# Expert 0 in two tiles of 128 rows, the first of them filled by batches 0 to 5 and computed while batch 7 is still being routed

## What is computed

```python
probs = softmax(x @ gate_w.T); w, idx = top_k(probs, 2); w = w / sum(w)
combine = zeros((T, E)).at[arange(T)[:, None], idx].add(w)
for gup, dn, ce in experts:                 # 8 experts, T = 896 tokens
    g, u = split(x @ gup.T, 2, axis=-1)     # 2 x 1024 columns
    acc += ce[:, None] * (silu(g) * u @ dn.T)
```

## Time and profile before

| | |
|---|---|
| runs shown | 602.05 us median of 3 (599.68 to 603.24) |
| the profiled execution | 603.49 us, its span 601.6 us |
| mean granted TensorE clock | 0.988 |
| TensorE busy | 573.0 us, 95% of the span |
| VectorE, ScalarE, GpSimd busy | 402.7, 313.5, 272.5 us |

### The profile page before, as it was taken

One profiled execution on the slowest core, in us unless ns is written; L12 is line 12 of the kernel. 1 busy time (PEld: TensorE's weight loads), 2 busy tenths in 40 slices (PEclk: granted clock), 3 DMA queues, 4 the chain that ended last, 5 costly groups with the idle time before them and its releaser, 6 DMA issues.

```text
span 601.6 us, 13755 instructions
## 1 busy us (share of the span) xinstructions
PE 573.0 (95%) x5612; PEld 488.8 (81%) x5612; DVE 402.7 (67%) x819; ACT 313.5 (52%) x601; POOL 272.5 (45%) x238
## 2 busy tenths in 40 slices
PE   7989999999989999999999999999899999999994
PEld 6767677777756887988888888867899999989994
DVE  7785577678686565667666676667586777746651
ACT  2434554555555556555565555544445567636641
POOL 4338468559641064546555564640300344421324
PEclk9989999999999999999999999998899999999998
DMA  7910480000000000000000000037172677636112
GB/s 233 360 45 3 173 322 2 2 3 1 3 2 1 2 1 2 9 1 24 17 9 17 9 25 1 23 130 307 32 232 85 233 244 254 211 71 225 30 20 25
DMA packets 23803, 50.93 MB, mean 85 GB/s; under 512 B 7040, under 2 KB 16560, under 8 KB 20400
## 3 DMA queue, kind: packets, MB, share of 16 engines
q1 hardware_dynamic: 18272, 45.20, 20.7%
q0 software_dynamic: 4224, 3.70, 3.4%
q10 hardware_dynamic: 1232, 1.01, 0.6%
HBM read 37.89 MB, written 13.31 MB: 85 GB/s over the span
## 4 chain that ended last, share of the span: by engine, by line
PE 83%; DVE 9%; POOL 3%; ACT 2%; issue 2%; DMA 1%; POOLq 0%; ACTq 0%; DVEq 0%
PE ps L59 14%; PE ps L60 13%; PE ps L61 13%; PE ps L736 5%; PE ps L705 5%; PE ps L718 4%; PE ps L593 4%; DVE KN L1103 4%; PE ps L574 3%; PE ps L665 3%; PE ps L655 2%; PE ps L609 2%; POOL sr L1796 2%; PE ps L553 2%; PE ps L485 1%
## 5 line engine op out<-in xcount | busy, mean ns | idle before, releaser
L1841 POOL TENSOR_SCALAR P<-P,rinv 112x487 f32<-112x487 f32 x56 | 84.5, 1521 | 62.7 <-DVE rinv L1136 62.5
L60 PE MATMUL ps<-XGf,WH 128*128 128x256 f32 x252 | 71.3, 283 | 0.0
L61 PE MATMUL ps<-XGf,WL 128*128 128x256 f32 x252 | 71.3, 283 | 0.0
L59 PE MATMUL ps<-XGf,WH 128*128 128x256 f32 x252 | 71.3, 283 | 0.0
L1796 POOL TENSOR_TENSOR sr<-sv,mhalf 125x32 f32<-125x32 f32 x13 | 70.7, 5436 | 1.1
L406 POOL DMA_INDIRECT out<-WS,rows_i x16 | 28.4, 1776 | 89.1 <-ACT WS L1696 85.7
L1103 DVE TENSOR_REDUCE KN<-ps 112x4 f32<-112x1500 f32 x32 | 55.0, 1717 | 19.2 <-PE ps L574 19.2
L1451 DVE TENSOR_TENSOR WL<-WR,WH 128x1024 fp32r<-128x1024 f32 x48 | 57.1, 1220 | 13.4 <-ACT WH L1750 9.8
L1612 ACT ACTIVATE P<-ps,nm 112x487 f32<-112x487 f32 x64 | 42.1, 663 | 45.4 <-DVE nm L1128 41.8
L1563 ACT ACTIVATE P<-ps 125x1344 f32<-125x1344 f32 x32 | 41.3, 1292 | 42.1 <-PE ps L593 42.1
L1128 DVE TENSOR_REDUCE nm<-ps 112x1 f32<-112x487 f32 x64 | 39.5, 658 | 17.3 <-PE ps L705 17.3
(11 more groups left out here) (268 smaller groups left out, 1556.8 us busy)
## 6 DMA issues: line engine op xcount, KB each, us to landing
WR<-in_gupT SPq DMA_DIRECT2D x16, 1024.0 KB, 6.6
WR<-in_dwnT SPq DMA_DIRECT2D x8, 1024.0 KB, 10.1
xs<-ZT SPq DMA_DIRECT2D x14, 516.0 KB, 5.7
CT<-in_ctxT SPq DMA_DIRECT2D x1, 2250.0 KB, 10.3
P<-xs SPq DMA_DIRECT2D x7, 256.0 KB, 10.7
P<-xs SPq DMA_DIRECT2D x9, 128.0 KB, 2.6
Wk<-in_L_xattn_Wk SPq DMA_DIRECT2D x2, 512.0 KB, 11.9
Wv<-in_L_xattn_Wv SPq DMA_DIRECT2D x2, 512.0 KB, 12.0
```

What stands on the lines that cost most here:

```text
L59: e.matmul(out, ah, bh, start=start, stop=False)
L60: e.matmul(out, ah, bl, start=False, stop=False)
L61: return e.matmul(out, al, bh, start=False, stop=stop)
L1841: e.tensor_scalar(P[:, k, 0:487], P[:, k, 0:487], rinv[:, k:k + 1], None, ALU.mult).then_inc(s("psc"), 1)
```

## The change

Expert 0 no longer runs as a pair of tiles. Its first tile is the first 128 rows of its stretch of `xs`. After batch 5 its count is raised to at least 128 (one VectorE instruction), so that later rows fall behind these; the scatters of batches 0 to 5 and of 6 and 7 have a semaphore each. SP loads the first tile when the former have landed (`early`, ahead of the loads of expert 1's weights in its queue). The tile's stages stand in the attention's order: `tx` (transposes, copy and low part), `tg` (four groups of six products of 512 columns, the rows stationary), `ts` (silu and product), `tt` (transposes back, copy and low part), `td` (24 products of 256 columns) and the scaled copy out. The second tile takes the same stages at the head of the expert part, with expert 1's transposes between them and expert 1's first unit ahead of its `td`. Expert 0's and expert 1's splits all move into the attention's order; pieces 3, 4 and 5 of expert 0's low parts go to GpSimd. The fillers of the former tail are gone, and 20 stand ahead of the second tile's transposes. The tables `PAIR_LAST`, `TAIL1`, `TAIL_NEXT` and `TAIL_LAST` have new times. Some semaphores are merged.

```diff
@@ tables
-SPLIT = ((10.5, "split", 0), (18, "low", 0), (38, "split", 1), (38.1, "split", 2), ...
+LOW_POOL = (3, 4, 5)
+SPLIT = ((7.66, "split", 0, 0), (10.03, "low", 0, 0), (10.22, "split", 0, 1), (12.31, "low", 0, 1),
...
+CUT, TILE = 6, 128
+EARLY = ((24.98, "tx"), (27.34, "tg", 0, 0), (29.62, "tg", 0, 1), (33.68, "tg", 1, 0), (37.84, "tg", 1, 1),
+         (33.8, "ts", 0), (35.59, "ts", 1), (42.7, "tt", 0), (48.77, "tt", 1), (93.43, "td"))
-WARM = {("kp", 0, 1, 0): 36, ("spk", 0, 2): 30, ("xt", NB - 1, 3): 18, ("rt4", NB - 1): 26, ("xin", 0): 62,
-        ("up", 0, 0): 10}
+WARM = {("tx", 1): 20, ("kp", 0, 1, 0): 36, ("spk", 0, 2): 30}
@@ expert_order
-    put("xin", 0)
+    put("tx", 1)
+    put("tg", 1, 0, 0)
+    put("tg", 1, 0, 1)
+    put("ts", 1, 0)
+    put("xin", 1)
+    put("tg", 1, 1, 0)
+    put("tg", 1, 1, 1)
+    put("ts", 1, 1)
+    put("tt", 1, 0)
+    put("pair", 2)
...
             put("up", x, dc)
+            if i == 0:
+                put("tt", 1, 1)
+                put("td", 1)
@@ TensorE, in tensor_first
+            if stage == "tx":
+                if t_ == 0:
+                    w.wait_ge(s("xg_early"), 16)
+                    w.wait_ge(s("aT1"), NB)
...
+                w.wait_ge(s("txh"), t_ + 1)
+                to = ps[:, 2 * q + part, :]
+                for z in range(2):
+                    o = z * 2048 + part * 1024 + q * 512
+                    w.wait_ge(*split_done(0, o // 1024))
+                    for W_ in W:
+                        e.matmul(to, XGTo[:, 0, z * 128:(z + 1) * 128], W_[:, o:o + 512],
+                                 start=(z == 0 and W_ is W[0]), stop=False)
+                w.wait_ge(s("txl"), t_ + 1)
...
         def tensor_experts(e, w):
-            w.wait_ge(s("prob"), 2 * NPAIR)
...
+            w.wait_ge(s("yc0"), 1)
@@ VectorE
+                if b == CUT - 1:
...
+                    e.tensor_scalar(base_[:, j, 0:1], base_[:, j, 0:1], float(TILE), None, ALU.max).then_inc(s("cut"), 1)
...
-            w.wait_ge(s("scatter"), 32 * NB)
-            for c in range(LATE_LOW, 4):
-                split_low(e, w, 0, c)
@@ GpSimd
+                elif stage == "low" and i[0] == 0 and i[1] in LOW_POOL:
+                    split_low(e, w, *i).then_inc(s("wl_pool"), 1)
@@ SP
+                elif stage == "early":
+                    w.wait_ge(s("scatter_a"), 32 * CUT)
+                    e.dma_start(XGe, xs[0:TILE, 0:D]).then_inc(s("xg_early"), 16)
+                    e.dma_start(EX[:, 0, 0, :], xs[0:TILE, D:ROW]).then_inc(s("wt_early"), 16)
```

More of the change, by code:

```diff
@@ L131 @@
          (22.8, "v1c", 2), (27.27, "v1c", 3))
[L132 to L146, removed]
+TAIL1 = ((12.93, "aT"), (13.76, "wo"), (14.9, "res", 3), (16.9, "stats", 3), (19.68, "norm", 3), (21.15, "xt", 3),
+         (20.64, "xtc", 3), (22.92, "rt0"), (23.2, "rt1"), (29.67, "rt2"), (32.6, "rt3"), (35.43, "rt4"),
+         (35.93, "rt5"))
@@ new lines @@
+TAIL_NEXT = ((13.99, "aT"), (16.94, "wo"), (16.89, "res", 3), (17.76, "stats", 3), (19.2, "norm", 3),
+             (24.91, "xt", 3), (23.91, "xtc", 3), (30.15, "rt0"), (24.95, "rt1"), (27.97, "rt2"), (28.8, "rt3"),
+             (33.27, "rt4"), (37.21, "rt5"))
+TAIL_LAST = ((-2.49, "rv"), (2.14, "rb"), (3.86, "rbc"), (3.57, "aT"), (13.1, "wo"), (9.19, "res", 3),
+             (10.9, "stats", 3), (12.24, "norm", 3), (16.34, "xt", 3), (16.47, "xtc", 3), (19.16, "rt0"),
+             (16.73, "rt1"), (18.97, "rt2"), (20.56, "rt3"), (28.06, "rt4"), (31.34, "rt5"))
@@ L216, in expert_order @@
     put = order.put
-    for x in range(2):
-        for c in range(3):
-            put("load", x, c)
+    for c in range(3):
+        put("load", 0, c)
+    put("early")
+    for c in range(3):
+        put("load", 1, c)
     put("pair", 0)
@@ L224, in expert_order @@
         put("load", 2, c)
-    put("xin", 0)
-    units = [(x, dc) for x in range(NE) for dc in range(4)]
+    put("tx", 1)
[8 more added lines that the diff above has]
+    put("pair", 2)
+    units = [(x, dc) for x in range(1, NE) for dc in range(4)]
     for i in range(len(units) + 2):
@@ L230, in expert_order @@
             put("up", x, dc)
-            if dc == 0 and x:
+            if i == 0:
+                put("tt", 1, 1)
+                put("td", 1)
+                put("rows", 0)
+                put("sent", 0)
+                put("over", 0)
+                put("oversent", 0)
+                put("ahead", 1)
+                for c in range(3):
+                    put("load", 3, c)
+            if dc == 0 and x > 1:
                 put("split", x, 5)
@@ L845, in tensor_experts @@
                         count.append(count_of(e, w, x))
[L846 to L850, removed]
+                    j, banks = x % 2, pair_banks(stage, x, dc)
+                    pair_free(w, stage, x, dc)
                     w.wait_ge(*pair_done("xin", x))
-                    for part in range(u == 1, 2):
+                    for part in range(2):
                         for c2 in range(2):
@@ L884, in tensor_experts @@
                     x, = i
+                    if x == 0:
+                        count.append(count_of(e, w, x))
                     with e.If(count[x] > 256):
@@ L918, in pairs_out @@
         def pairs_out(w, x):
+            w.wait_ge(s("ttl"), 4)
             before = [pair_use[q] for q in moe.entries[:moe.entries.index(("over", x))] if q in pair_use]
-            for k in range(3):
-                w.wait_ge(s(f"pair{k}"), 1 + max(u // 3 for u in before if u % 3 == k))
+            for k in range(4):
+                w.wait_ge(s(f"pair{k}"), max([n for j, n in before if j == k], default=0))
         def sent_before(w, x, k):
             if k:
-                w.wait_ge(s(f"far_y{x}"), 16 * k)
+                w.wait_ge(s("far_y"), 64 * x + 16 * k)
             else:
```

337 lines of the change are left out of this document (222 added, 115 removed).

## The result

| | before | after |
|---|---|---|
| time, median of 8 runs each | 601.94 us (599.68 to 603.62) | 606.27 us (604.69 to 609.54) |
| ratio, 95% interval | | 1.0093, 1.0068 to 1.0117 |
| the profiled execution, its span | 603.49, 601.6 us | 608.78, 607.0 us |

The change makes the kernel slower by 4.3 us; the prediction was 598.5. The profiled execution of after is 2.5 above its median, so its rows show one of the bad cases.

A forecast was written before the change was run, and what follows sets the result against it. It took the chain of waits from the last attention product (418.00) to expert 0's first (440.09) as the bound. Dense work gave gain 448.35 - t; with t 444.9, 3.5 us off the 602.05 median: 598.5, range 596.5 to 600.5.

The forecast's parts named there:

- rival 3: GpSimd's three 3.0 us pieces and VectorE exclude each other: half blocked 603.1, in full 607.6; chance 0.12.
- both of its signs: Signs that the forecast is wrong: t past 447, and VectorE's low parts over 1.22 us beside GpSimd's.
- t: Time of the second tile's first product, taken as 444.9; the change gains 448.35 - t.
- How much work leaves the dense part: From the second tile's first product to expert 2's transposes: 18.26 us, so without delay the gain would be 8.2.
- (a) to (c): Chain through batch 7's norm and routing: row numbers 4.6 us late, scatters landed at 440.7, t not before 443.9.
- 1.0 that I had added for `td`'s clock: Allowance for the early tile's down products partly at half clock, moving t from 443.9 to 444.9.
- (b): Batch 7's norm to its first routing instruction: VectorE's 3.04 us outlasts TensorE's 1.40 us group; routing starts at 428.4.
- (d): Early tile's down products, fillers and transposes: t 443.7 at full clock, up to 2.9 us more at half speed.
- GpSimd's pieces: Three low parts of expert 0 on GpSimd, priced 3.0 us each from bounds of 2.9 and 3.2.
- What costs nothing: ScalarE's four splits, GpSimd's low parts, expert 1's rows, the count's `max` and merged semaphores: covered or small.
- rival 2: Gain lost to late early rows or earlier batches' tails stalling TensorE (3 us): 601 to 602; chance 0.21.
- Rival 1: VectorE's additions hide in waits: row numbers 1.5 us late, t about 441.5, gain 6.8, time 595.2; chance 0.17.

The follow-up runs named there:

- e5: The changed kernel with GpSimd's three two-input subtractions replaced by one-input multiplications of the same columns, those low parts left out: 601.99 us, ratio 0.9985 to 1.0018.
- e9: The changed kernel with VectorE/GpSimd instruction pairs measured ahead of it: VectorE's two-SBUF-input instruction took 2.00 us beside a subtraction, 0.74 multiplication, 0.68 copy, 0.42 base.
- e12: The kernel before, with only three GpSimd multiplications of 1024 columns added in the places of the change's three pieces: 602.48 us, ratio 0.9987 to 1.0021.
- e2: The changed kernel with piece 3 of expert 1's low parts moved behind batch 7's row numbers on VectorE: 606.51 us, ratio 1.0048 to 1.0078.
- e3: The changed kernel with GpSimd's pieces on VectorE, expert 1's last three low parts behind the scatters' landing, 8 last fillers for 20: 601.82 us, ratio 0.9976 to 1.0011.
- e4: The changed kernel with 20 fillers added on TensorE ahead of the early tile's second group of transposes: 608.61 us, ratio 1.0061 to 1.0131.
- e10: The changed kernel with pieces 3 and 4 on VectorE and only piece 5 left on GpSimd: 605.10 us, ratio 1.0031 to 1.0067.
- e7: e3 with batch 7's row numbers put directly behind its choice on VectorE: 601.34 us, ratio 0.9974 to 1.0012.

## Why the prediction was wrong, by its steps

**The step that failed is the weighing of one row against rival 3.** Rows 9 showed a two-input VectorE instruction inside one of GpSimd, not held up, and I took this for GpSimd in general. That instruction of GpSimd is a multiplication, the one form that lets VectorE through (e5, e9, e12); the change adds subtractions. I did note that no row showed two two-input instructions together, and still gave the case 0.12. What the runs show in its place: beside a subtraction of 1024 columns VectorE's two-input instruction takes 2.00 us instead of 0.42 (e9), its low part 3.70 instead of 1.22 (after), and the form alone makes 4.3 us (e5). Rival 3 had the mechanism: VectorE's chain was blocked for 6.1 us in the profiled execution, past the 3.5 at which it said that blocking decides, and both of its signs came (t at 453.2, past 447; low parts of 2.85 and 3.70). That its range, 603.1 to 607.6, holds the median 606.3 is in part luck. It adds the blocking to a 598.5 that was itself 3.5 us too low, as e5 shows (602.0 without the blocking), and the clock that fell behind the blocking is not in it. Of the 7.8 us between 598.5 and 606.3 the blocking with what follows from it explains 4.3.

**How much work leaves the dense part:** 18.26 predicted, 18.67 measured (453.16 to 471.83). Nearly right. That the clock may be low at its start, 1.6 us more, was missed; it happened in e2, e3, e4 and e10.

**(a) to (c), the chain to the row numbers.** Norm 7 was to end at 425.4 and ended at 429.9, the routing was to start at 428.4 and started at 433.9, the first row numbers were to come at about 436.0 and came at 443.9. With the multiplication in the subtractions' place (e5) root 6 to the first product is 32.3 us; the prediction's 444.9 - 413.6 is 31.3. Up to the end of the first row number it is 23.2 in e5 and 22.4 in the sum, so VectorE's additions were right within 1 us. Behind it two errors nearly cancel, by luck: the scatter's 1.25 (2.19 for 0.94, in e5 too), which I did not have, and 1.0 that I had added for `td`'s clock, while e5's TensorE waits 1.47 for the rows and `td` is not on its path. VectorE's low parts behind the row numbers had no price in my sum, since nothing in VectorE's queue waits for them, but they hold up GpSimd.

**(b), the clock.** That TensorE's clock falls earlier, behind the wait for norm 6, was not foreseen. The six products ahead of `rt0 7` took 2.7 us at a granted clock of 0.50 instead of 1.40, and VectorE waited 1.08 for them.

**(d)** `td` at half speed was foreseen (2.9 to 5.8 us); it took 5.3. In after it ended 0.3 ahead of the rows' path, with its fillers; it decided only when the rest was mended (e7).

**GpSimd's pieces** take 2.35 us, not 3.0: both my bounds were too high, the time per column of a multiplication is no bound for a subtraction.

**What costs nothing:** the earlier batches' tails cost 0.8 us (aligned), a quarter of what rival 2 allowed. Rival 2's early rows were in time: their load was issued at 410.7 and landed 2.0 later, and their transposes at 421.30 waited for VectorE. Rival 1 did not come about.

What e5 gives against before is less than its path says: 32.3 against 34.7, less 0.4 in the dense part and 0.8 to 1.2 up to root 6, leaves about 1 us of gain, and none was measured. So of the 3.5 us by which the forecast was off without any blocking, about 2.5 are found (1.0 between root 6 and t, 0.4, 0.8 to 1.2), and 1 stays open.

## What to carry to other kernels

An idle GpSimd is not free help for a busy VectorE: before work is moved there, list what VectorE runs beside it, and let that be instructions that read PSUM or reduce (unchanged beside all three forms in e9). A row shows the absence of a conflict only for its own two forms. And low-priority work directly behind the instruction that releases a scatter is not free either: put it behind the landing. Last, a chain that is shortened brings the clock of the idle engine onto the path, so fillers that cost nothing before are worth trying again.

## What was not expected of the hardware

- GpSimd's instruction on SBUF holds VectorE up by form: a 1024-column subtraction (2.34 us) and copy (1.04 us) until they end, a multiplication (2.77 us) by 0.2 to 0.3 us, 0.7 in e12. On GpSimd the copy is 2.7 times as fast as the multiplication.
- VectorE's instruction that began first is not always safe: the low part at 437.86 began 0.26 before GpSimd's piece and took 3.70. But in e4 the low part at 417.16 began 0.07 before GpSimd's pair and took its usual 1.21, while the pair took 5.69 instead of 4.71. The order of the starts in the trace does not tell which of the two waits.
- A scatter's issue on GpSimd (0.94) is held up by VectorE's subtractions in SBUF for as long as they follow one another: 2.22 beside two, 3.35 beside three, 0.94 beside none. The Trainium skill, in the section named above, infers that a `tensor_tensor` does not hold up the making of descriptors; in these rows the whole issue is held up; which part of it waits they do not show.
- The granted clock between 24 and 44 us is 0.91 in some profiled executions and 1.00 in others, though all these programs do the same there. With it the landmark at 44.1 moves by 1.4 us.
